# Identity transposes by PE in front of waits, in a one-core kernel of four attention and four feed-forward layers

## What is computed

```python
x = x + _L0_xattn_ref(_layernorm(x, axis=-1), ctx_2048, itok_BxS_0_1023, ...)   # latent attention, 16 heads of 128 + 64
x = x + _L0_ffn_ref(_layernorm(x, axis=-1), ...)      # 8 experts, 2 per token, and a shared part
x = x + _L1_xattn_ref(_layernorm(x, axis=-1), ctx_2048, mask_BxS2_ik0, ...)     # 16 heads of 32, scores clipped
x = x + _L1_ffn_ref(_layernorm(x, axis=-1), ...)      # quantised weights and activations
x = x + _L2_xattn_ref(_layernorm(x, axis=-1), ctx_2048, ...)                    # 16 heads of 32, softmax
x = x + _L2_ffn_ref(_layernorm(x, axis=-1), ...)      # gated, inner width 2048
x = x + _L3_xattn_ref(_layernorm(x, axis=-1), ctx_2048, ctx_2048, ...)          # linear attention, feature maps
x = x + _L3_ffn_ref(_layernorm(x, axis=-1), ...)      # 16 experts, 4 given per token
```

## Time and profile before

| | us |
|---|---|
| median of 3 timed runs | 2352.18 (2352.13 to 2353.78) |
| the profiled execution | 2344.26 |
| its span, first to last instruction | 2342.4 |
| PE busy | 2071.5 |
| PEld, DVE, ACT, POOL busy | 1668.7, 1086.6, 910.5, 495.7 |
| share of PE in the chain that ended last | 67% |
| mean granted TensorE clock | 0.946 |

### The profile page before, as it was taken

One profiled execution on the slowest core, in us unless ns is written; L12 is line 12 of the kernel. 1 busy time (PEld: TensorE's weight loads), 2 busy tenths in 40 slices (PEclk: granted clock), 3 DMA queues, 4 the chain that ended last, 5 costly groups with the idle time before them and its releaser, 6 DMA issues.

```text
span 2342.4 us, 39238 instructions
## 1 busy us (share of the span) xinstructions
PE 2071.5 (88%) x14719; PEld 1668.7 (71%) x14719; DVE 1086.6 (46%) x2401; ACT 910.5 (39%) x1738; POOL 495.7 (21%) x358
## 2 busy tenths in 40 slices
PE   5989999897896798996878999799978999989996
PEld 5976666687444777784567777799977999845554
DVE  4447677565113255678725666423242555511111
ACT  3246556533221354556644555422243322222221
POOL 3233232231231311100031010033221111023332
PEclk7889999999898899997989999999998999989998
DMA  3210010125324221131010000122220100389995
GB/s 109 59 39 26 14 39 1 41 81 208 134 90 128 80 72 64 54 141 59 4 62 23 27 26 2 46 68 63 62 62 29 35 26 13 120 252 323 322 323 151
DMA packets 90860, 203.68 MB, mean 87 GB/s; under 512 B 9198, under 2 KB 14418, under 8 KB 88594
## 3 DMA queue, kind: packets, MB, share of 16 engines
q1 hardware_dynamic: 80562, 174.82, 22.8%
q0 software_dynamic: 10144, 26.75, 4.3%
HBM read 183.84 MB, written 19.53 MB: 87 GB/s over the span
## 4 chain that ended last, share of the span: by engine, by line
PE 67%; DMA 11%; DVE 9%; ACT 7%; issue 5%; POOL 1%; SPq 0%; ACTq 0%; DVEq 0%; POOLq 0%
PE psum L106 15%; PE psum L107 14%; PE psum L109 13%; DMA l3f_sum_dram<-l3f_y,l3f_rows 8%; PE psum L887 3%; PE psum L3466 2%; PE psum L2696 2%; PE psum L3436 2%; PE psum L2119 1%; PE psum L913 1%; PE psum L2924 1%; PE psum L1528 1%; PE psum L3452 1%; PE psum L2346 1%; DVE l2x_highest L2201 1%
## 5 line engine op out<-in xcount | busy, mean ns | idle before, releaser
L1528 PE MATMUL psum<-l3f_gate_up,l3f_x_turned 128*128 128x352 f32 x496 | 153.4, 463 | 0.8 <-ACT l3f_x_turned L1587 0.8
L1528 PEld LDWEIGHTS psum<-l3f_gate_up,l3f_x_turned 128*128 128x128 f32 x496 | 92.6, 192 | 47.7 <-issue 1.2
L3225 POOL TENSOR_TENSOR l0x_w_lo<-l0x_w_raw,l0x_w_hi 128x512 fp32r<-128x512 f32 x52 | 71.9, 1401 | 150.6 <-ACT l0x_w_hi L3478 126.2
L2160 ACT ACTIVATE l2x_probs<-psum,l2x_shift 100x361 f32<-100x361 f32 x128 | 64.9, 559 | 97.4 <-DVE l2x_shift L2205 96.2
L3580 ACT ACTIVATE l0x_probs<-l0x_probs,l0x_lowest 100x361 f32<-100x361 f32 x128 | 75.1, 588 | 59.9 <-DVE l0x_lowest L3744 59.7
L106 PE MATMUL psum<-xn_hi,l2f_w_gu_hi 128*128 128x400 f32 x256 | 90.4, 353 | 8.9 <-ACT l2f_silu L588 4.9
L1803 POOL TENSOR_TENSOR l2x_ctx_lo<-l2x_ctx_raw,l2x_ctx_hi 128x1448 fp32r<-128x1448 f32 x8 | 26.3, 3287 | 325.1 <-ACT l2x_ctx_hi L1811 325.0
L107 PE MATMUL psum<-xn_lo,l2f_w_gu_hi 128*128 128x400 f32 x256 | 89.4, 349 | 0.0
L1503 POOL DMA_INDIRECT l3f_sum_dram<-l3f_y,l3f_rows x31 | 49.2, 1587 | 179.6 <-DMA l3f_sum_dram<-l3f_y,l3f_rows 140.4
L1613 DVE TENSOR_TENSOR l3f_h<-l3f_silu,psum 128x352 f32<-128x352 f32 x31 | 16.2, 522 | 151.1 <-ACT l3f_silu L1600 151.1
L1554 PE MATMUL psum<-l3f_down,l3f_h_turned 128*128 128x512 f32 x186 | 85.1, 593 | 0.8 <-DVE l3f_h_turned L1619 0.8
(11 more groups left out here) (533 smaller groups left out, 6153.1 us busy)
## 6 DMA issues: line engine op xcount, KB each, us to landing
l3f_gate_up<-in_slabs_dram SPq DMA_DIRECT2D x31, 1280.0 KB, 8.1
l3f_down<-in_slabs_dram SPq DMA_DIRECT2D x31, 512.0 KB, 5.4
l0x_w_raw<-in_slabs_dram SPq DMA_DIRECT2D x52, 256.0 KB, 2.8
l0f_weights<-in_slabs_dram SPq DMA_DIRECT2D x8, 1536.0 KB, 17.5
l1x_piece<-in_bit_w_dram SPq DMA_DIRECT2D x8, 1024.0 KB, 6.5
l1f_raw<-in_bit_w_dram SPq DMA_DIRECT2D x8, 1024.0 KB, 8.9
l2f_raw_gu<-in_slabs_dram SPq DMA_DIRECT2D x32, 256.0 KB, 2.6
l3f_down<-in_slabs_dram SPq DMA_DIRECT2D x31, 192.0 KB, 7.1
```

What stands on the lines that cost most here:

```text
L1528: mm = pe.matmul(c.psum[:, bank + x, 0:self.INNER], self.x_turned[:, t % 2, k, :], self.gate_up[:, q, at:at + self.INNER], start=k == 0, s ...
L2160: act.activation(self.probs[:, m % 2, g, :], c.psum[0:S, g, 0:C], ACT.Exp, bias=self.shift[:, g:g + 1], scale=self.SCALE).then_inc(self.s( ...
L3225: pool.tensor_tensor(self.w_lo[:, place, :], self.w_raw[:, n % 3, :], self.w_hi[:, place, :], ALU.subtract).then_inc(self.s("w_split"), 1)
```

## The change

A new helper makes PE turn the 128 x 128 identity, `count` times, into the four quarters of one bank. Nobody reads the result, and the next product that uses the bank overwrites it. The helper has no semaphore of its own: the transposes run as soon as PE comes to them. Each call stands ahead of the wait of the instruction that follows.

```diff
+def keep_busy(c, pe, bank, count):
+    for x in range(count):
+        pe.transpose(c.psum[:, bank, x % 4 * P:(x % 4 + 1) * P], c.identity[:, :], c.identity[:, :])
@@ RoutedFfn.pe_sum (l0f)
         pe.wait_ge(self.s("added"), u + 1)
+        if m == 0:
+            keep_busy(c, pe, self.LAST_BANKS[u], 36 if h else 40)
@@ RoutedFfn.pe (l0f)
         wait_for_input(c, pe, self, 4)
+        keep_busy(c, pe, 0, 24)
         self.pe_shared(c, pe, 0, 0)
...
         self.pe_tables(c, pe)
+        keep_busy(c, pe, 1, 50)
@@ ChosenFfn.pe (l3f)
         pe.wait_ge(c.sem("ln_rows"), self.norm.before + self.norm.batches)
+        keep_busy(c, pe, 4, 52)
         self.pe_turn_x(c, pe, 0)
...
         self.pe_down(c, pe, self.TILES - 1)
+        keep_busy(c, pe, 4, 80)
         pe.wait_ge(self.s("sum_landed"), 16 * self.groups)
@@ Attention.pe (l1x, l2x, l3x)
         n.back(pe, 0)
         n.back(pe, 1)
+        keep_busy(c, pe, 4, 28)
         self.pe_keys(pe, 0, 0, 0)
@@ Attention.pe_start (l1x, l2x)
+        keep_busy(c, pe, 4, 10)
         pe.wait_ge(self.s("q_copied"), KD)
@@ Attention.pe_batch (l2x)
             i = b * 4 + m
+            if m == 0 and isinstance(b, int) and b == 0:
+                keep_busy(c, pe, 4, 14)
@@ LinearAttention.pe_start (l3x)
+        keep_busy(c, pe, 4, 22)
         pe.wait_ge(self.s("maps_lo"), 1)
@@ LatentAttention.pe_batch (l0x)
             wait(pe, self.s("turned_01"), i)
+            if m == 0:
+                keep_busy(c, pe, 4, 5)
```

## The result

The changed kernel is slower. The median of its 8 timed runs is 2360.23 us (2356.77 to 2371.35), that of the kernel before beside them 2349.49 us; the ratio is 1.0046, 95% interval [1.003, 1.0061], so +7 to +14 us. A second series, timed with the experiments, gave 1.0031 [1.0018, 1.0043].

The account below looks back on a forecast made before the run. PE was taken to bound the kernel, busy 88% of the span, losing time to waits and half-clock work behind them. Delays of 9.6 us against gains of 9.5 us gave 2352.3 us, no change; range 2344.5 to 2360.

Parts of the forecast that it names:

- The 28 at the heads: Heads of l1x, l2x, l3x: 28 transposes lie in no wait and delay each stage 3.1 us, +9.2 us in all.
- The two cancel: At the heads, fillers at half clock cover half-clock time of the keys, so the net delay is 28 at full-clock price.
- The l0x term: l0x: five fillers per batch keep the clock in three batches that lost it, -4.5 us; overrun in the last, +0.4 us.
- PE waits for DVE's probabilities at the start of a batch: 8 waits: l0x: 12.8 us of waits together, seven of 1.7 to 2.1 us, the last batch's only 0.2.
- A wait of 1.2 us should keep it nearly always: l0x: with the fillers in the wait, batches nearly always keep full clock, -4.5 us for the three that lost it.
- A lost clock costs 1.5 us here: l0x: a batch that loses its clock takes 1.5 us longer, nearly what half clock costs PE.
- The starts: Fillers in waits of l2x, l1x and l3x, predicted to gain -1.8, -0.9 and -1.0 us.
- l0f and l3f: Long waits: l0f's first product -0.8 us, its sums -0.5, nothing at l0f's first gather, l3f's first rows and last sum.
- Those start at full clock: Fillers 50, 52 and 80 would overrun their waits at half clock, but start at full clock, so none overruns.
- The sum: Whole kernel: delays 9.6 us against gains 9.5 us, the time staying within 0.1 us; chance 0.50.
- The second: Rival: idleness left still costs the clock; gains only 2.5 to 3 us, the 28s stay, +6.8, 2359 us; chance 0.20.
- The third: Rival: transposes don't hold the clock, the skill's rule; no gain, +24, 2377 us; chance 0.03.

Follow-up runs that it names:

- e4: Kernel before plus only five transposes per l0x batch at head group 3, where the 1.7 us wait is: 0.9991 [0.998, 1.0002], -2.1 us.
- e8: Kernel before plus only 14 transposes ahead of head group 3 of each l0x batch: 0.9997 [0.9986, 1.0007], -0.7 us.
- e5: Kernel before plus only the fillers ahead of first scores and feature maps (10 in l1x, 10 and 14 in l2x, 22 in l3x): 0.9981, -4.5 us.
- e3: Kernel before plus only five transposes at head group 0 of each l0x batch, as in the change: 0.9998 [0.9989, 1.0007], -0.5 us.
- e6: Kernel before plus only the l0f and l3f fillers (24, 50, 40, 36; 52, 80): 0.9984 [0.9972, 0.9996], -3.8 us.
- e14: Kernel before plus the 28 transposes at three heads and the l0f and l3f fillers: 1.0024 [1.001, 1.0038], +5.6 us.
- e11: Changed kernel, the 28s replaced by 44 ahead of the first turn back, behind a residual wait, in l1x, l2x, l3x: 0.9942, -13.6 us against before.
- e1: Changed kernel without the 28 transposes at the heads of l1x, l2x and l3x: 0.9978 [0.9969, 0.9987], -5.2 us against the kernel before.
- e12: Kernel before, PE's residual wait moved ahead of its first turn back in l1x, l2x and l3x, no filler: 1.0002 [0.9988, 1.0016].
- e10: Kernel before plus fillers at all places, larger counts, the heads' moved behind a residual wait, 44 ahead of the first values: 0.9952, -11.3 us.
- e13: As e10, but none ahead of the sums, 20 for the values' 44, 34 for l3f's 36: 0.9923, median 2330.13 us, -18.1 us against before.

## Why the prediction was wrong, point by point

- **The 28 at the heads, +9.2 us: right**, and measured at +10.6 [7.1, 14.1]. The picture was as predicted: no idle time ahead of them, both waits as long as before, the stretch to the values longer in all three stages. The price per head was 3.1 to 4.2 us, not 3.1; in l2x and l3x 0.7 to 1.7 of it came back by the end of the values. "The two cancel" was a little off: the 28 took 5.43 us in l1x and 4.84 in l2x, so many of them ran at half clock.
- **The l0x term, -4.5 + 0.4 us: wrong in place.** "PE waits for DVE's probabilities at the start of a batch: 8 waits" is the step that failed. The earlier trace rows give a line and a count, not a head group, and I put the eight waits at `m == 0`, because eight batches fit eight waits. Only batch 0's are there; six are at `m == 3`, and the short one of 0.2 us isn't the last batch's but a second one of batch 0. So seven of the eight fillers stood in no such wait, and two batches lost their clock, as before. "A wait of 1.2 us should keep it nearly always" fell, too: five transposes in the right place left 1.17 us, and the same clocks were lost (e4). "A lost clock costs 1.5 us here" held: where fourteen kept two clocks (e8), the trace gained 1.5 us at each, and gave 2.0 back at the two passes that have no wait. Measured: -0.5 us [-2.6, +1.6] for the term as it was built.
- **The starts, -3.7 us: right in number**, -4.5 [-6.3, -2.4], but not in each part. In e5's trace l2x gave its 1.8 us, and there is no half clock there between 1226 and 1240 us, in the changed kernel neither. l3x gave 0.4 (1.7 in the changed kernel) for my 1.0. In l1x I find nothing of the 0.9: with 1.44 us of idleness left the scores ran at full clock and half clock followed from 822 us on, as in e3 and e4, which have no filler there. That the sum came out is in part luck.
- **l0f and l3f, -1.3 us: right in sign, too small**, -3.8 [-6.6, -0.9]. I gave nothing for l3f's 52. "Those start at full clock" was wrong of them: a third of the wait that I counted for them (3.5 of 9.9 us) lies ahead of them, they start at half clock and overrun by 1.6 us; the turn and the products behind them run at full clock and give 2.0 us back, 0.3 to 0.4 net. The rest of the 3.8 us I can't place: at l0f's first product, its first gathered rows and its sums, and at the last sum, e6's trace isn't ahead of e3's, which has no filler there.
- **The sum.** Mine was +0.1. With the measured parts it is 10.6 - 0.5 - 4.5 - 3.8 = +1.8, with the 28s and all the rest together 10.6 - 5.2 = +5.4, and the whole measured +10.8 [7.1, 14.3] and +7.3 [4.2, 10.1]. So the l0x term was off by 3.6 us, the largest of the four, the 28 by 1.4, and the starts and l0f and l3f by -3.3 together. Some 2 to 9 us stay open, and part of that may be the spread of the parts: their four intervals together make about 5 us either way. I first thought that the parts disturb each other, but e14 and e11 add up within their intervals. Half clocks do fall on the path in places without any filler, as that at the end of l2x. The traces show one more place: in l0f the stretch with the wait for the first gathered rows grew by 2.5 to 3.1 us in both traces of the changed kernel and in e1's and e11's, against 0.1 and 0.4 us in e6's and e14's, which have the same fillers in l0f. But e8's trace has 3.0 us there without any filler in l0f. What either place has to do with the open part isn't shown.
- **The rivals.** The second came nearest, 2359 us: little gain from l0x, the 28s stay, and its point of decision was gains under 4.9 us; they measured 5.2. Its reason, that the idleness left still costs the clock, held in l0x (e4). That its number comes so near is luck: it had gains of 2.8 us and delays of 9.6, the runs have 5.2 and 10.6, and their sum leaves the same open part as mine. The third fell: 80 transposes alone took 0.11 us each, and the window over them has a granted clock of 1.00. The Trainium skill, TensorE: Matmul & The Clock Gate, Part 4, says that full clock doesn't engage for transpose mode; here it stayed under 80 of them and rose under the 52, from the first of these windows to the second. For these transposes of float32 the measurement decides against that sentence.

```profile
2349.70:2358.50 8.80, 8.80 (x81) 8.64 (x79) 0.00 (x0) 0.69 (x1) 1.55 (x1) 1.00 0.41 58
...
2077.20:2081.60 4.40, 4.40 (x21) 4.40 (x22) 0.00 (x0) 0.00 (x0) 0.66 (x1) 0.50 0.58 197
2081.70:2085.00 3.30, 3.30 (x33) 3.30 (x32) 0.00 (x0) 0.00 (x0) 2.14 (x3) 1.00 0.55 148
```

## What to carry to other kernels

A filler pays only where it stands inside the wait that it is meant to fill: ask of each call which semaphore PE waits for just behind it, and whether the trace shows idle time right behind it, not merely near it. Fill the wait nearly to its end, counting at half-clock price where idleness precedes the filler; overruns cost nearly in full (28 behind a wait 3.1 to 4.2 us, 14 in a pass without one 1.3 to 1.4), and the same 44 transposes were worth -8 us in one wait and nothing in the next. A table of waits by line doesn't tell which pass of a loop waits: look at the timeline of every kind of pass, the last ones too, before you place or price an edit in the loop.

## What the runs showed of the hardware

I had not expected that a higher mean clock and a busier PE could go with a slower kernel, nor that so short a rest of idleness decides in l0x: in the same two batches 1.17 us left (and 1.72 us without a filler there) went with half clock and 0.18 us with full. It isn't a fixed limit: in before's trace batches 1, 3, 4 and 6 kept the clock with the whole wait.

Nor are they always the same batches. In the fourteen traces without the fillers of 14 the half clocks of l0x's batches came in only two patterns: in batches 2 and 5 (at 233 and 339 us) or in 3 and 5 (at 269 and 341 us). e12 shows the other one than before, though the two kernels don't differ up to there. The pattern went with the time at which the program came to l0x (167 us in before): 0 to 1.6 us later than before's in the seven traces of the first, 1.9 to 2.5 us later in the seven of the second. The three traces with 14 ahead of the wait (e8, e10, e13) show neither.
